# Routing weights of two expert mixtures spread over the partitions by DMAs instead of by TensorE

## What is computed

```python
# L0_ffn, second half: 8 experts of 256 hidden, top 2, one shared expert of 256 (not weighted)
combine = sum(one_hot(topi, 8) * softmax(topw)[..., None])           # [tokens, 8]
shared = swiglu(h2, sh_gate, sh_up, sh_down)
eout = (silu(h2 @ e_gate) * (h2 @ e_up)) @ e_down                    # each expert
moe_out = shared + sum_e eout[e] * combine[:, e]

# L1_ffn: 16 experts of 64 hidden, top 2, one shared expert of 256, weighted by a sigmoid
y = sum_e ((silu(x @ We_gate[e].T) * (x @ We_up[e].T)) @ We_down[e].T) * weight[:, e]
y = y + sigmoid(x @ Wsg.T) * (silu(x @ Ws_gate.T) * (x @ Ws_up.T) @ Ws_down.T)
```

## Time and profile before

| | |
|---|---|
| median of three runs | 496.0 us |
| span of the profiled execution | 494.2 us |
| around it (difference of the two) | 1.8 us |
| TensorE busy | 453.3 us, 92% |
| VectorE / ScalarE / GpSimd busy | 72% / 58% / 65% |
| matmuls of L1930 (weights over the partitions) | 68 |

### The profile page before, as it was taken

How to read it: one execution, slowest core, us unless ns; L and a number is a source line. 1 busy time by engine, 2 the same in 40 slices (tenths; PEclk the granted TensorE clock), 3 DMA queues, 4 the chain that set the end, 5 groups by cost and what they waited for, 6 DMA issues and landing times.

```text
span 494.2 us, 11017 instructions
## 1 busy us (share of the span) xinstructions
PE 453.3 (92%) x3724; PEld 341.0 (69%) x3724; DVE 358.1 (72%) x930; ACT 287.7 (58%) x559; POOL 319.0 (65%) x525
## 2 busy tenths in 40 slices
PE   6859888999999999999999999899989997899996
PEld 5646555676677777677767877686858775687674
DVE  4657877899988878968656747775766756877864
ACT  2424566766787774565674476536664477446452
POOL 7895889898868676546934584547635573446553
PEclk9988999999999999999999999999999999999999
DMA  6340000040101000020000000000000000000000
GB/s 164 79 140 2 0 3 3 1 119 5 56 3 57 1 1 0 1 55 0 2 1 0 2 1 1 0 0 0 0 0 1 2 1 0 23 1 23 0 23 21
DMA packets 19353, 9.80 MB, mean 20 GB/s; under 512 B 6535, under 2 KB 18792, under 8 KB 19304
## 3 DMA queue, kind: packets, MB, share of 16 engines
q1 hardware_dynamic: 18584, 9.04, 6.9%
q10 hardware_dynamic: 720, 0.13, 0.2%
HBM read 8.12 MB, written 1.05 MB: 19 GB/s over the span
## 4 chain that ended last, share of the span: by engine, by line
PE 49%; POOL 18%; DVE 14%; issue 13%; ACT 4%; POOLq 1%; ACTq 0%; DVEq 0%
PE PS L1774 9%; PE PS L1776 9%; PE PS L1775 8%; POOL HLO L618 3%; DVE work L1382 2%; PE PS L1700 2%; PE PS L1694 2%; PE PS L1930 2%; DVE work L1387 2%; PE PS L1689 2%; PE PS L1662 2%; PE PS L1734 2%; POOL rs L437 1%; DVE RDT L1135 1%; PE PS L1677 1%
## 5 line engine op out<-in xcount | busy, mean ns | idle before, releaser
L618 POOL TENSOR_TENSOR HLO<-work,HHI 128x512 fp32r<-128x512 f32 x111 | 143.1, 1292 | 128.2 <-ACT HHI L869 124.8
L876 ACT ACTIVATE work<-PS 128x512 f32<-128x512 f32 x112 | 66.8, 596 | 91.1 <-PE PS L1776 88.4
L1382 DVE TENSOR_TENSOR work<-work,PS 128x512 f32<-128x512 f32 x104 | 71.0, 683 | 57.3 <-ACT work L876 32.3
L1387 DVE TENSOR_TENSOR work<-PS,work 128x512 f32<-128x512 f32 x112 | 77.2, 691 | 19.2 <-POOL HLO L618 10.8
L869 ACT ACTIVATE HHI<-work 128x512 fp32r<-128x512 f32 x111 | 69.8, 629 | 29.3 <-DVE work L1387 29.1
L1099 DVE TENSOR_REDUCE nmax<-PS 128x4 f32<-128x512 f32 x64 | 42.2, 683 | 8.3 <-PE PS L1662 7.9
L738 ACT ACTIVATE EX<-PS 128x512 f32<-128x512 f32 x64 | 35.0, 603 | 12.3 <-PE PS L1677 12.1
L1774 PE MATMUL PS<-HHI,W0H_down 128*128 128x512 f32 x72 | 35.0, 485 | 0.2
L1774 PE MATMUL PS<-H2H,W0H_gate 128*128 128x512 f32 (+1 forms) x72 | 32.0, 444 | 0.7 <-ACT work L876 0.7
L1930 PE MATMUL PS<-CWT,sel 128*128 128x512 bf16 (+1 forms) x68 | 26.5, 390 | 6.5 <-DVE work L1382 6.0
L1774 PE MATMUL PS<-H2H,W0H_up 128*128 128x512 f32 (+1 forms) x72 | 29.2, 406 | 2.9 <-DVE work L1387 2.9
(11 more groups left out here) (355 smaller groups left out, 1204.3 us busy)
## 6 DMA issues: line engine op xcount, KB each, us to landing
X<-in_x_dram SPq DMA_DIRECT2D x4, 256.0 KB, 5.2
raw<-in_L_ffn_e_gate_dram SPq DMA_DIRECT2D x1, 1024.0 KB, 5.5
raw<-in_L_ffn_e_up_dram SPq DMA_DIRECT2D x1, 1024.0 KB, 7.2
out_dram<-X SPq DMA_DIRECT2D x3, 256.0 KB, 2.3
raw<-in_L_ffn_We_gate_dram SPq DMA_DIRECT2D x1, 512.0 KB, 4.0
raw<-in_L_ffn_We_up_dram SPq DMA_DIRECT2D x1, 512.0 KB, 3.9
raw<-in_L_ffn_We_down_dram SPq DMA_DIRECT2D x1, 512.0 KB, 4.1
ctx_nat<-in_ctx_dram SPq DMA_DIRECT2D x1, 462.0 KB
```

Of the source, the lines that this page charges most:

```text
L618: pool.tensor_tensor(HLO[t][:], HH[k % 2][:], HHI[t][:].bitcast(F32), ALU.subtract).then_inc(m_sem["lo"], 1)
L876: act.activation(SG[c % 2][:], PS[:, c % 2, :], ACT.Silu).then_inc(S["silu"], 1)
L1382: dve.tensor_tensor(SG[c % 2][:], SG[c % 2][:], PS[:, 4, :], ALU.mult).then_inc(S["scaled"], 1)
L1387: dve.tensor_tensor(HH[c % 2][:], PS[:, 2 + c % 2, :], SG[c % 2][:], ALU.mult).then_inc(S["hid"], 1)
```

## The change

The selectors, the three pieces and the 68 matmuls go. `comb` is now transposed in float32 to [experts, tokens], and copied to `CW` in SBUF (17 x 512). SyncE's queue stores it to a DRAM tensor `WD` (`store_rows`), and then loads each expert's row of 512 weights back with a source that repeats it over the 128 partitions, into one of four buffers `BCW` (`spread_weights`). A load waits until VectorE has done with the buffer's last user. VectorE's multiplication reads `BCW` (SBUF) instead of PSUM. The first mixture works on the shared expert's two chunks first, which need no weight. There are 32 loads of one row repeated 128 times in the first mixture; in the second 32 loads of two rows, each repeated 64 times, and 4 of one row repeated 128 times.

```diff
+    UNWEIGHTED = (2, 0)
+    WD = [nc.dram_tensor(f"WD{m}", (G, E, GT), F32) for m, E in enumerate((E0, E1 + 1))]
...
-        CS = sb("CS", [P, B, P], BF16)
-        sel0 = sb("sel0", [P, E0, P], BF16)
-        sel1 = sb("sel1", [P, NC1 + 1, P], BF16)
+        CW = sb("CW", [E1 + 1, GT])
+        BCW = [sb(f"BCW{r}", [P, GT]) for r in range(RING)]
...
+        def weights_of(m, c):
+            return (c - 2) % NCH[0] if m == 0 else c
+        def load_of(m, c):
+            return (c - 2) // 2 if m == 0 else min(c, NC1)
...
+            def store_rows(m, g):
+                sp.wait_ge(r_sem[m]["ct_sb"], g + 2)
+                sp.dma_start(WD[m][g], CW[0:(E0, E1 + 1)[m], :]).then_inc(rows_out, 16)
+            def spread_weights(m, g):
+                sp.wait_ge(rows_out, 16 * (m * G + g + 1))
+                for e in range(NBC[m]):
+                    k = g * NBC[m] + OFF[m][2] + e
+                    if k >= RING:
+                        sp.wait_ge(m_sem["scaled"], last_use(k - RING) + 2)
+                    if m == 0:
+                        what = WD[0][g, e:e + 1, :].broadcast_to([P, GT])
+                        sp.dma_start(BCW[k % RING][:], what).then_inc(spread[k % RING], 16)
+                    elif e < NC1:
+                        what = WD[1][g, 2 * e:2 * e + 2, :].unsqueeze(1).broadcast_to([2, F1, GT])
+                        sp.dma_start(BCW[k % RING][:], what).then_inc(spread[k % RING], 16)
+                    else:
+                        what = WD[1][g, E1:E1 + 1, :].broadcast_to([P, GT])
+                        sp.dma_start(BCW[k % RING][:], what).then_inc(spread[k % RING], 16)
...
                 else:
+                    store_rows(0, 0)
+                    spread_weights(0, 0)
+                    store_rows(0, 1)
                     sp.wait_ge(turn_ps, 3)
...
+            store_rows(0, 2)
+            store_rows(0, 3)
+            spread_weights(0, 1)
+            spread_weights(0, 2)
+            store_rows(1, 0)
+            spread_weights(0, 3)
+            store_rows(1, 1)
+            spread_weights(1, 0)
             for g in range(G - 1):
+                spread_weights(1, g + 1)
+                if g + 2 < G:
+                    store_rows(1, g + 2)
                 sp.wait_ge(m_sem["x"], G + g + 2)
                 sp.dma_start(out[g * GB:(g + 1) * GB].rearrange("b s d -> s b d"), X[:, g * GB:(g + 1) * GB, :]).then_inc(out_done, 16)
...
-            step(pool.memset(CS[:].bitcast(F32), 0.0))
...
-            def turned_weights(k, bank, lo, n):
+            def turned_weights(k, bank):
                 act.wait_ge(r_sem[0]["ct"], k + 2)
-                act.activation(CWT[:, lo * P:(lo + n) * P], PS[:, bank, 0:n * P // 2].bitcast(BF16), ACT.Copy).then_inc(r_sem[0]["ct_sb"], 1)
+                if k >= 1:
+                    act.wait_ge(rows_out, 16 * k)
+                act.activation(CW[0:E0, :], PS[0:E0, bank, :], ACT.Copy).then_inc(r_sem[0]["ct_sb"], 1)
...
                 def ct_sb():
                     act.wait_ge(r_sem[1]["ct"], g + 2)
-                    act.activation(CWT[:, bass.ds(g * GT, GT)], PS[:, 5, 0:GT // 2].bitcast(BF16), ACT.Copy).then_inc(r_sem[1]["ct_sb"], 1)
+                    act.wait_ge(rows_out, g * 16 + 16 * G)
+                    act.activation(CW[:], PS[0:E1 + 1, 5, :], ACT.Copy).then_inc(r_sem[1]["ct_sb"], 1)
...
-                        dve.wait_ge(S["bc"], g * NBC[m] + OFF[m][2] + e + 2)
-                        dve.tensor_tensor(SG[c % 2][:], SG[c % 2][:], PS[:, 4, :], ALU.mult).then_inc(S["scaled"], 1)
+                        dve.wait_ge(spread[r], 16 * uses)
+                        dve.tensor_tensor(SG[c % 2][:], SG[c % 2][:], BCW[r][:], ALU.mult).then_inc(S["scaled"], 1)
...
-                for j in range(n):
-                    ins = pe.transpose(PS[:, bank, :].bitcast(BF16)[:, j * P:(j + 1) * P], CS[:, lo + j, :], identb[:])
+                for j in range(GB):
+                    ins = pe.transpose(PS[0:E0, bank, j * P:(j + 1) * P], comb[:, k * GB + j, 0:E0], identf[:])
...
-                    if first_of_expert(m, c):
-                        e = c // per
...
-                        pe.wait_ge(S["scaled"], g * NSC[m] + OFF[m][1] + e * per + 1)
-                        pe.matmul(PS[:, 4, :], SEL[m][:, e, :], CWT[:, bass.ds(g * GT, GT)], start=True, stop=True).then_inc(S["bc"], 1)
```

More of the change, by code:

```diff
@@ L200, in stage @@
             return made
-        gates_in, bias_in, small_in, wkv_in, wa_in, wb_in, wr_in, wqv_in = (
-            sem(n) for n in ("gates_in", "bias_in", "small_in", "wkv_in", "wa_in", "wb_in", "wr_in", "wqv_in"))
+        gates_in, bias_in, small_in, wkv_in, wa_in, wb_in, wr_in = (
+            sem(n) for n in ("gates_in", "bias_in", "small_in", "wkv_in", "wa_in", "wb_in", "wr_in"))
         x_in = [sem(f"x_in{g}") for g in range(G)]
         ctx_in = [sem(f"ctx_in{k}") for k in range(2)]
-        raw_in = [sem(f"raw_in{k}") for k in range(6)]
+        raw_in = [sem(f"raw_in{k}") for k in range(3)]
         halved = sem("halved")
@@ L211, in build @@
         out_done = sem("out_done")
+        rows_out = sem("rows_out")
+        spread = [sem(f"spread{r}") for r in range(RING)]
         a_sem = {n: sem(f"a_{n}") for n in ("t", "kv", "kq", "v2", "s", "pt", "y", "y_half", "xt", "kq_sb", "v2_sb", "e", "pt_sb",
@@ L221, in build @@
         r_chain = [sem(f"r{m}_chain") for m in range(2)]
-        m_sem = stage("m", pe="bc g u down yn", act="silu hi yt", dve="scaled hid x st", pool="lo yx")
+        m_sem = stage("m", pe="g u down yn", act="silu hi yt", dve="scaled hid x st", pool="lo yx")
         c_sem = stage("c", pe="t s bt at bbt hq hc o", act="xn e3 xt exp bexp at_sb hq_sb",
@@ L479, in _, with expert_numbers @@
                 bias_group(g)
[L481 removed]
+            def expert_numbers():
                 pool.iota(iota_i[:], pattern=[[1, E1]], base=0, channel_multiplier=0).then_inc(pool_c, 1)
                 n[0] += 1
[L484 to L494, removed]
[L495 to L501 removed]
+                pool.wait_ge(pool_c, n[0])
+                pool.tensor_copy(iota_e[:], iota_i[:]).then_inc(consts, 1)
             n0 = NC0 + 2
@@ L528, in halves_of_weights @@
                 if b == 1:
[L529 to L531 removed]
+                    expert_numbers()
                 for k, c in pieces[max(b - 3, 0) * per_batch:max(b - 2, 0) * per_batch if b < B - 1 else len(pieces)]:
@@ L1322, in two_largest, with places_of_two @@
                 C(dve.tensor_copy(topf[:, 0:nb, :], topi[:, 0:nb, 0:2]))
-            def places_of_two(m, C, nb):
+            def places_of_two(m, g, C, nb):
                 E = (E0, E1)[m]
-                dve.wait_ge(consts, 3)
+                if isinstance(g, int) and g == 0:
+                    dve.wait_ge(r_sem[0]["ct"], G + 1)
+                dve.wait_ge(r_sem[m]["ct"], g + 1)
                 io = iota_e[:, 0:E].unsqueeze(1).broadcast_to([P, nb, E])
@@ L1337, in weighted_places @@
                     C(dve.tensor_tensor(to, to, wsel[:, 0:nb, k:k + 1].broadcast_to([P, nb, E]), ALU.mult))
-                C(dve.tensor_tensor(cm, cm, ct, ALU.add))
+                dve.tensor_tensor(cm, cm, ct, ALU.add).then_inc(r_sem[m]["cs"], 1)
+                C.end()
             def differences_of_two():
@@ L1351, in weights_of_two @@
                 C(dve.tensor_scalar(w1, w1, 0.5, 0.5, ALU.mult, ALU.add))
-            def in_pieces(m, g, C, nb):
-                R, E = r_sem[m], (E0, E1)[m]
-                EW = E + m
-                dve.wait_ge(R["ct"], g + 1)
-                cf = comb[:, 0:nb, 0:EW]
-                for p in range(3):
-                    piece = CS[:, 0:nb, p * PIECE:p * PIECE + EW]
-                    ins = dve.tensor_copy(piece, cf)
-                    if p == 2:
-                        ins.then_inc(R["cs"], 1)
-                    else:
-                        C(ins)
-                        C(dve.tensor_tensor(cf, cf, piece, ALU.subtract))
-                C.end()
             S = m_sem
```

108 lines of the change are left out of this document (43 added, 65 removed).

## The result

The changed kernel takes 572.0 us (median; 571.5 to 572.77) against 496.0 for the kernel before on the same chip. The ratio is 1.153, 95% interval 1.151 to 1.155. The forecast was 569. The profiled execution has a span of 570.3 us, 1.7 under its time.

What follows compares the result with a forecast made beforehand. TensorE was taken to bound the kernel before. Loads start at 369.5 - 9 = 360.5 us; two-engine loads of 5.5 us bring the span to 567, plus 1.8: 569 us. Range 547 to 600 (0.73), 540 to 650 for 8 in 10.

Steps and rivals of the forecast that it cites:

- The division of a load: Second-mixture loads: two source rows outermost, each repeated 64 times, put a load on two engines, 64 packets of 2 KB each.
- rival A: Second-mixture loads run on 16 engines after all, so every chunk is covered: 480 us, chance 0.15.
- rival B: Second-mixture loads: one engine needs 129 ns for 2 KB, 86 us more: 655 us, chance 0.08.
- The time of a load: Second-mixture loads: 85 ns per 2 KB packet, 5.5 us a load, with 4.8 and 8.2 us kept beside it.
- The second mixture, step by step: Span clock from 360.5 us through four groups' stores and loads to the end at 567; 206 us instead of 125.
- The lead at the start of it: At the copy of group 1's second-mixture weights the changed kernel is ahead by 9 us, between 3 and 14.
- the 4 us of the attention: Before the first mixture: GpSimd loses selectors and clearing, at most 4.6 us on the path, taken as 4.
- The matmuls, their waits and the transposes: First mixture: 7.4 us of selector matmuls and 2 us of waits saved, 1 us lost to float32 transposes.
- The exclusion: First mixture: VectorE's multiplication with two SBUF operands and GpSimd's L618 lengthen each other; 0 to 19 us, taken as 3.
- the sign that I had named: First mixture must be at TensorE's pace, 2.1 us a chunk where nothing is inserted.
- rival C: Loads on 16 engines, but VectorE and GpSimd hold each other up, 31 us more: about 510 us, chance 0.04.
- the border before the last group: Second mixture with quick loads: store, load and copy take 7 us against TensorE's 4.9 of products ahead; 3 us added.

Runs made afterwards that it cites:

- the run with four loads: The changed kernel with only the first four weight loads, all later ones left out (wrong weights): 489.5 us, ratio 0.986.
- the run with the operand in PSUM: The changed kernel with only the first four loads, VectorE's multiplication reading PSUM bank 4 instead of the SBUF buffer (wrong weights): 476.0 us, ratio 0.958.
- the run with both operands in SBUF: The changed kernel with only the first four loads, VectorE's multiplication still reading two SBUF operands (wrong weights): 489.5 us, ratio 0.986.
- The halves: The changed kernel with each second-mixture load issued as two, each one row repeated over 64 partitions, all computed: 495.7 us, ratio 0.998.
- the single row: The changed kernel with each second-mixture load repeating one row over 128 partitions (half of its weights wrong): 495.3 us, ratio 0.997.
- the last two runs: Changed kernel with half loads and silu written back to PSUM: 486.6 us; the same without the last group's weight store (wrong weights there): 478.8 us.

## Why the prediction was right, and where it wasn't

**The division of a load.** Right, and shown. A load has two small packets, not 16, and keeps 2.08 engines busy; rival A (480 us, 16 engines) falls by the kernel after, rival B (129 ns a packet) by the spacing of 5.35 us. VectorE waits 3.5 us a chunk for its load (106.4 in 30), where I wrote some 3. The step had been taken from transfers whose destination had as many rows as the source; the runs with one and four rows close this gap. No row of before shows that small packets count engines; the shares of the runs do (2.08 and 4.13 engines for two and four). Nor does a row show the store of the 17 rows on one engine, which the sum has at 1.5 us. In the run with four loads that store stands alone: 367 to 371 us have 18 packets, one of them small, at 2.9% of 16 engines, that is 1.9 us of packet time. So the number of outermost rows is not the count in every transfer: those 17 left one small packet, the 8 rows of the first mixture's store left eight (16 packets, 8 of them small, in 167.4 to 168.85 us of the kernel after).

**The time of a load.** Forecast 5.5 us, measured 5.35; forecast 85 ns a packet, measured 84. Carrying the rows of 512 B and 1 KB on by another 18.9 ns was sound. The bound of 129 ns from packets written in 512 B pieces was far off, and the shorter time for a load that I kept beside the sum, 4.8 us, was too short.

**The second mixture, step by step.** Counted from the store of group 1's weights (367.03; forecast 360.5):

| | forecast | measured |
|---|---|---|
| first load of group 0 in use | 9.5 | 8.9 (375.94) |
| eighth load of group 0 | 48.0 | 46.4 (413.38) |
| eighth load of group 1 | 92.7 | 89.9 (456.89) |
| first load of group 2 | 104.4 | 99.5 (466.49) |
| eighth load of group 2 | 142.9 | 137.7 (504.72) |
| first load of group 3 | 157.8 | 154.4 (521.39) |
| eighth load of group 3 | 196.3 | 191.8 (558.84) |
| end | 206.5 | 203.3 (570.3) |

(The forecast's 453.9 for group 1 has the shared row's 0.7 us in it; it is taken off here.) Seven loads were 1.1 us shorter than forecast in groups 0 and 3 (37.4 instead of 38.5). The gap from group 2's last to group 3's first load was 16.7 instead of 14.9, since the copy came 5.3 us after the last multiplication (510.01) and not 3.3.

**The lead at the start of it: wrong.** Forecast 9 us, with 3 to 14 as its bounds; measured 369.03 - 366.44 = 2.6, under the lower bound. The terms: the 4 us of the attention were 3.2 (169.95 - 166.78), or less by the spread of this copy told above. The matmuls, their waits and the transposes, 7.4 + 2 - 1 = 8.4, were 8.5 together: that is what the first mixture gained in the run with the operand in PSUM (199.1 - 190.6). It holds whatever else the change does there too, the order of the chunks among it; no run measures the transposes by themselves. But their starts are 0.11 us apart in the kernel after: from the first of four to the next group of matmuls it is 0.44 us onto 8 partitions (165.36) and onto 17 (309.78), and 0.43 onto 128 (165.80). That is less than the 0.23 that I had as the bound, though not for the reason that I gave, the few partitions. The exclusion, costed at 3 us, was 9.1 (199.7 - 190.6), and 8.0 when it alone was added to the kernel before. 3.2 + 8.5 - 9.1 = 2.6. So the sign that I had named, the first mixture at TensorE's pace, did not come: TensorE was busy for 48.1 of 53 us there.

So the step that failed is the size of one term: "but VectorE idles a third of its time there and the products run three chunks behind, so 3 us". The mechanism was right, and the bounds of 0 to 19 us held the value; I went toward the low end by an average of idle time. Idle time is no cover for it, since the two instructions don't start at random. ScalarE writes the silu of a chunk and right behind it the high part of the chunk before (`chunks`: the silu, then `leading(c - 1)`). So VectorE's multiplication for the one and GpSimd's low part for the other become ready almost together, and TensorE waits for the work behind both. The trace of the kernel before had this already:

```profile
303.40 0.67 DVE L1382 TENSOR_TENSOR work<-work,PS 128x512 f32<-128x512 f32 x1
303.86 1.29 POOL L618 TENSOR_TENSOR HLO<-work,HHI 128x512 fp32r<-128x512 f32 x1 [1.14 <-ACT HHI L869]
```

Of the 64 multiplications of its first mixture 50 overlap an L618, for 16.5 us together. That count, and not the idle share, was the number to start from. In the kernel after, up to the copy of group 1's weights, TensorE waits 5.4 us for GpSimd's low part and 5.9 for VectorE's product; up to 360 us the run with both operands in SBUF has 5.4 and 5.1, and the one with PSUM 1.3 and 3.8. These rows make 5.4 of the 9.0 us between the two runs; the rest is spread over waits that I haven't itemised.

**The two errors met.** The store came 6.5 us later than forecast (367.03 instead of 360.5); the loads' steps and the end took 3.2 off: 570.3 instead of 567 for the span. So the forecast was right by the term that carried it (30 waits, 106 us), and that it came within 3 us owes something to luck: without the second error the first alone would have made it 6.5 us.

**Rival A, had it come true.** I gave it 480 us. The halves and the single row are that case, and took 495.7 and 495.3: outside of what I gave A, within 0.5% of the kernel before, halfway to rival C's 510. The span forecast was 478, measured 494.4. The exclusion was 12.8 (the spans of the two runs with four loads are 487.2 and 474.4) and not the 3 + 2 costed, 7.8 more; the border before the last group was 7.8 and not 3, 4.8 more. That makes 12.6 of 16.4; the rest, some 4 us, isn't settled. Had the loads run on 16 engines, my range would have missed, and my "faster" for that case would have been wrong. A rival's price deserves the same work as the forecast's.

**The clock.** I wrote that TensorE had 3.4 us a chunk to lose (5.5 less 2.1) before its clock counts. Within a group that held: at 0.83 (mean of the second mixture) VectorE still waits for the load. At a border it counts, as the last two runs show for a kernel with quick loads (0.64 in 457 to 466 us and 25 matmuls, against 1.00 and 43). In the kernel after this share wasn't measured by itself.

## What to carry to other kernels

Look at the outermost size of a repeated source before all else: here one row repeated had 16 small packets, with a share of 0.99 of 16 engines, and two rows had two, with 0.130. The pair took 5.35 us a load; as two DMAs of one row each the same bytes landed 3.0 us after their issue, and VectorE waited three times instead of 30. When an operand moves from PSUM to SBUF, ask which VectorE and GpSimd instructions then both read SBUF, count in the timeline how often they overlap, and don't let idle shares speak it away: here it cost 10.8 to 13.5 us over 104 instructions, 0.10 to 0.13 us each. Writing the partner operand back into its PSUM bank took it away (693 ns for the longest multiplication instead of 1796). The round through DRAM (copy, store, load) before the last group, with three chunks of work ahead of it, cost 7.8 us: TensorE stood still for 4.7 us and then ran at a granted clock of 0.64 for nine us.

## What the runs showed of the hardware that I had not expected

SyncE's own issue was held. In the kernel after, the loads and what stood behind them on the queue (start, us):

```profile
367.37 31.55 SPq L332 DMA_DIRECT2D BCW<-WD  x8
398.96 5.19 SPq L335 DMA_DIRECT2D BCW<-WD  x1
404.27 38.02 SPq L332 DMA_DIRECT2D BCW<-WD  x8
442.34 5.59 SPq L335 DMA_DIRECT2D BCW<-WD  x1
448.73 0.25 SPq L318 DMA_DIRECT2D WD<-CW  x1
```

An issue took 5.18 us (median), as long as a load, though each of these loads had a free buffer to go to, since SyncE waits for the buffer ahead of the DMA; L335, one row repeated 128 times, took 5.2 to 5.9 us as well, behind the others. With two buffers the same DMA was issued in 0.475 us, with four rows in 0.50, with one row in 0.32. So it seems to be the loads outstanding in a queue that hold the issuing engine itself. The first four issues of group 0, each from a window of its own, show from which one on:

```profile
367.37 0.61 SPq L332 DMA_DIRECT2D BCW<-WD  x1
368.02 0.54 SPq L332 DMA_DIRECT2D BCW<-WD  x1
368.61 2.67 SPq L332 DMA_DIRECT2D BCW<-WD  x1
371.32 6.53 SPq L332 DMA_DIRECT2D BCW<-WD  x1
```

Two loads of 64 packets an engine went out at once, the third was held; at 459.92, the third of group 2, it was 2.51 us again. What exactly fills up isn't shown. No cost of it shows here: the copies that the next stores wait for came at 448.13 and 510.01, when SyncE was free again, and the ring of two, whose issues aren't held, was no faster. The output's stores landed 10.4 us after their issue (median), where they took 2.3 in the kernel before and 5.6 with the ring of two.
